# Constant matmuls in TensorE's pauses at the borders of the spectral stage and of the last stage of a four-layer convolution kernel

## The reference, cut to what matters

```python
x = x + _L0_conv_ref(_gn(x), ...)   # 1x1 channel mixing, leaky relu, then (y - min) / (max - min) per channel
x = x + _L1_conv_ref(_gn(x), ...)   # rfft2, a 3x3 complex convolution over the frequencies, bias, irfft2
x = x + _L2_conv_ref(_gn(x), ...)   # x rounded to int8 steps, 3x3 convolution, scale and bias
x = x + _L3_conv_ref(_gn(x), ...)   # circular 3x3 convolution
```

## Time and profile before

| what | value |
|---|---|
| time, median of 3 runs | 6660.71 us (6643.02 to 6668.57) |
| the profiled execution: its own time | 6655.92 us |
| its span, first to last instruction | 6653.9 us |
| TensorE matmul busy | 5695.1 us, 86% |
| VectorE busy | 4982.8 us, 75% |
| ScalarE busy | 4486.0 us, 67% |
| mean granted TensorE clock | 0.952 |

### The profile page before, as it was taken

The page is one execution under the profiler, slowest core; times in us unless marked ns, Lnnn a source line. Parts: engine busy times, 40 slices in busy tenths (PEclk is TensorE's granted clock), DMA queues, the critical chain, the costliest instruction groups (busy, mean ns, idle before and its releaser), DMA issues. The chain is left out here.

```text
span 6653.9 us, 202054 instructions
## 1 busy us (share of the span) xinstructions
PE 5695.1 (86%) x64138; PEld 3662.2 (55%) x64138; DVE 4982.8 (75%) x9849; ACT 4486.0 (67%) x8680; POOL 2750.1 (41%) x4633
## 2 busy tenths in 40 slices
PE   0259989989988988988998997994889889889889
PEld 0027757757756766765775774872334334334334
DVE  6867887887887887877887887788667667667664
ACT  0367766766767767767766556555878778778776
POOL 2136555556556646546556555650111111111112
PEclk9979999999999999999999998998999999999999
DMA  5325634633643652651661551553667667667665
GB/s 177 121 59 151 185 101 129 185 123 110 185 141 92 186 159 74 185 177 56 184 188 35 143 140 38 143 143 60 170 164 202 166 172 207 170 163 207 165 173 137
DMA packets 535618, 959.15 MB, mean 144 GB/s; under 512 B 121946, under 2 KB 126682, under 8 KB 532826
## 3 DMA queue, kind: packets, MB, share of 16 engines
q1 hardware_dynamic: 471898, 815.99, 44.0%
q10 hardware_dynamic: 63104, 134.23, 6.5%
HBM read 560.66 MB, written 287.60 MB: 127 GB/s over the span
## 5 line engine op out<-in xcount | busy, mean ns | idle before, releaser
L1575 PE MATMUL pC<-xs,taps 128*128 128x512 f16 x4608 | 1094.2, 382 | 108.1 <-DMA xhalo<-xs 100.4
L872 PE MATMUL pM<-gw,xh 64*128 64x256 f16 (+1 forms) x24960 | 1126.1, 244 | 0.0
L872 PEld LDWEIGHTS pM<-gw,xh 64*128 64x128 f16 x24960 | 964.6, 95 | 129.1 <-issue 2.9
L607 POOL TENSOR_TENSOR X<-X,zo 128x256 f32 (+1 forms) x512 | 371.9, 726 | 1243.5 <-DVE X L1019 1243.5
L1575 PEld LDWEIGHTS pC<-xs,taps 128*128 128x128 f16 x4608 | 448.4, 98 | 670.9 <-DVE xs L1624 88.3
L1471 POOL TENSOR_TENSOR xn<-xn,one_col 128x1 f32<-128x1 f32 x520 | 175.2, 337 | 1367.4 <-ACT xn L1505 1367.4
L778 PE MATMUL pM<-X,mix0s 64*64 64x512 f32 x2304 | 533.1, 638 | 179.8 <-DVE X L991 108.2
L592 POOL TENSOR_TENSOR X<-X,rl 128x512 f32 x384 | 478.2, 1274 | 397.0 <-ACT rl L638 396.7
L1491 ACT ACTIVATE scaled<-X,qbias,qscale 128x512 f32 (+1 forms) x512 | 410.9, 804 | 338.8 <-DMA X<-after_layer 277.8
L1513 ACT ACTIVATE xs<-xn 128x1028 f16<-128x1028 f32 x520 | 545.7, 1049 | 89.3 <-POOL xn L1472 88.7
L1019 DVE SCALAR_TENSOR_TENSOR X<-pZ,X 128x512 f32 (+1 forms) x512 | 353.8, 691 | 327.6 <-ACT zo L667 326.4
(11 more groups left out here) (236 smaller groups left out, 13781.1 us busy)
## 6 DMA issues: line engine op xcount, KB each, us to landing
gw<-row_weights SPq DMA_DIRECT2D x520, 288.0 KB, 3.4
after_layer<-X SPq DMA_DIRECT2D x512, 256.0 KB
out_dram<-result SPq DMA_DIRECT2D x512, 256.0 KB
stage<-in_x_dram SPq DMA_DIRECT2D x224, 512.0 KB
X<-in_x_dram SPq DMA_DIRECT2D x448, 256.0 KB
X<-after_layer ACTq DMA_DIRECT2D x224, 512.0 KB, 5.7
xhalo<-xs SPq DMA_DIRECT2D x504, 96.4 KB, 3.8
qhalo<-q SPq DMA_DIRECT2D x496, 96.2 KB, 4.0
```

The lines of the kernel that those rows point to most:

```text
L607: nc.gpsimd.tensor_tensor(X[:, j, 0], X[:, j, 0], zo[:, k], ALU.add)
L872: nc.tensor.matmul(pY[:, r, col:col + nd * P], row(xh, r)[:, k, p, ri, off:off + P], weights(r, q_, d, nd, ri), start=ri == 0 and off == 1 ...
L1575: nc.tensor.matmul(bank, taps3[:, d, wh], xs[:, h, own, d:d + W], start=d == 0 and n == 0, stop=False)
```

## The change

A helper `warm` is added to each of the two TensorE programs: n matmuls on constant operands that wait for no semaphore and set none. In the first program they read the table `inv_odd` and write half a bank of `pT` or `pZ` (a half that the next real matmul into it starts anew); in the second they read the weights `taps3` and write a new bank, `pIdle`, that nothing reads. Real matmuls, other engines and DMAs stay as they are. The places:

- 12 matmuls (256 columns) ahead of `small(n)` of each image,
- 40 (256 columns) between `mix(b, 3)` and `mix(b, 4)`,
- 36 (256 columns) behind `small(n + 3)`, ahead of the first transpose,
- 2 (512 columns) behind each of the conv2 of tiles 54 to 63, where conv3 has no tile any more,
- 8 (512 columns) ahead of the statistics matmul of the second program and 36 behind it.

```diff
+                    def warm(bank, n):
+
+                        for _ in range(n):
+                            nc.tensor.matmul(bank, inv_odd[:, 0, 0, 0:P], inv_odd[:, 0, 1], start=True, stop=True)
...
                         n = b * SMALL + 2
+                        warm(pT[:, HALF:W], 12)
                         small(n, pS[0:2, 0:P], ext[:, :], ident[:, :])
                         small(n + 1, pS[:, 0:2], ext_rows[:, :], ident[0:2, 0:2])
                         for j in range(J):
+                            if j == 4:
+                                warm(pT[:, HALF:W], 40)
                             mix(b, j)
...
                         small(n + 3, pS[:, 1:2], gmean1[:, :], mv[:, 1:2])
+                        warm(pZ[:, HALF:W], 36)
                         for i in range(ITEMS + 3):
...
+                pIdle = ps("pIdle", [P, W], pm)
...
+                    def warm(n):
+
+                        for _ in range(n):
+                            nc.tensor.matmul(pIdle[:, :], taps3[:, 0, 0], taps3[:, :, :].rearrange("p d h o -> p (d h o)")[:, 0:W],
+                                             start=True, stop=True)
+
                     def stats(b):
+                        warm(8)
                         pe.wait_ge(stats_in, b + 1)
                         nc.tensor.matmul(pS[:, 0:2], gmean2[:, :], mv[:, :], start=True, stop=True).then_inc(stats_out, 1)
+                        warm(36)
...
                             if c2 and live(w, 0, J):
                                 conv2(b + 1, w, k, g)
+                                if isinstance(v, int) and v > J:
+                                    warm(2)
```

## The result

The changed kernel takes 6691.3 us (median of 5 runs, 6689.1 to 6706.8), the kernel before 6660.7 us in its 5 runs. The ratio is 1.0051, with a 95% interval of 1.0031 to 1.0071. That lies in the predicted range of 6638 to 6700 us, but 23 us above the point of 6668, and at the border of what was called no change.

What follows compares the result with a forecast made beforehand. TensorE was taken to bound the steady parts, VectorE the mixing, and chains through other engines the borders. The terms +24.5 - 10 - 2 = +12.5 us on 6655.9 us gave 6668.4 us, range 6638 to 6700 us.

Steps and rivals of the forecast that it cites:

- What bounds the kernel: TensorE sets the pace in the steady parts, VectorE in mixing without slack, chains through other engines at the borders.
- The twelve: Ahead of `ext`: they take 2.5 us at the low clock, hidden in the wait with 0.5 us left.
- The credit for the clock at `ext`: The clock may rise inside the twelve, quickening the small matmuls and first tiles: 0 to 0.6 us an image.
- The forty: Between mixing tiles 3 and 4: not hidden, +3.5 us in seven images, +24.5 us; bounds +10 to +32.
- The rival in which they are hidden: Mixing tile 4 was late anyway, so only the gains stay: 6644 us; chance 0.10 together with no effect.
- the rival of low-clock fillers: Fillers run at the low clock, the forty +55 us, sum 6726 us; chance 0.16 with other costs of that size.
- The thirty-six at the spectral start: Ahead of the first transpose: no cost, 1.2 us gained an image, -10 us in all; bounds -23 and 0.
- 2.8 us: that is the most: Spectral start followed step by step at the high clock: first products end 2.8 us sooner, the most an image gains.
- The row that was called to agree: An image with a 10.2 not 13.6 us low stretch reached the next `ext` in 420.74 not 423.50 us.
- The last stage: Fillers behind each late conv2 and around the statistics: -2 us for the whole stage; bounds -18 and +15.
- The sum: All places together: +24.5 - 10 - 2 = +12.5 us, giving 6668.4 us.
- The rule: Half of all low-clock time counts as lost, whatever the engine does: 639 us of low clock cost 320 us.

Runs made afterwards that it cites:

- no_forty: The changed kernel without the forty fillers between mixing tiles 3 and 4: 6664.6 us (11 runs), ratio 1.0008 to the kernel before.
- edge: The changed kernel without the forty, the twelve moved to the end of the loop's body, ahead of its branch: 6650.3 us, one run.
- hold: The changed kernel without the forty, 54 instead of 36 fillers ahead of the first transpose, 12 and 5 more in the next two pauses: 6654.2 us, one run.
- first_only: The changed kernel with only the first program's fillers (12, 40 and 36), the second program as before: 6681.6 us (5 runs), ratio 1.0037.
- last_only: The changed kernel with only the second program's fillers, the first program as before: 6658.9 us (11 runs), ratio 1.0006.
- combo_border: The changed kernel without the forty; 54, 12, 5 at spectral start, 54 behind second-program statistics, pauses around an image's last pairs filled: 6626.9 us, ratio 0.9948.

## Why the prediction was right or wrong, point by point

**What bounds the kernel** held: steady parts kept their pace, and a delay of VectorE in the mixing stage went onto the end (no_forty).

**The twelve: this step failed.** The prediction said "hidden, with 0.5 us left", from a pair that ends and a wait that follows. The twelve start 1.86 us behind the pair in place of at once, so they end 1.4 us behind `ext`. In the kernel before, the same delay at the loop's end lay unseen inside the wait of 3.10 us for `ext`: the trace gave the wait its last releaser, and I took the whole of it for room. At the first border that trace shows idle time of this kind bare (the row at 924.27), and I had not read it. It cost +9.2 us, where the sum had none; edge shows it by moving the twelve ahead of the branch. The credit for the clock at `ext` was right: no_forty's mixing is (597.5 - 592.7) / 7 = 0.7 us shorter an image than before, and hold's, with the same twelve, less than 0.1 us (597.2), against 0 to 0.6.

**The forty** were right in mechanism and nearly in size: +24.5 us forecast, +21.3 with the credit in it measured (+27.6 in first_only's trace, where the clock was low at `ext` in five of the seven images and not in two). The rival in which they are hidden is out (26 us by no_forty), and the rival of low-clock fillers too, in which they cost +55. Both clocks at `ext` occur: with it low, 89.5 to 90.5 us; with it high, 87.6 to 87.8, +2.5 on 85.2 and not the +1.4 that the prediction had for that case. The forty start 5.0 us behind `ext`'s matmul there (4.55 forecast), take 4.54 us (4.4), and VectorE's second group starts 1.24 us behind the start of tile 4's matmuls (0.96). So the second group comes 10.72 us behind `ext`'s matmul, against 8.49 before and 12 in the forecast; with the clock low it comes 12.8 to 13.5 us behind. The first image shows nothing (136.6 for 136.3 us), as said.

**The thirty-six at the spectral start**: -10 us forecast, -3.2 measured, with the wait of 2.32 us behind them as forecast. For a pause left open 1.2 us an image was too much: 0.4 measured in this profile, and 0.4 to 0.9 over the six profiles that have this filler. For a start wholly at the high clock, "2.8 us: that is the most" was too little: 3.4 in six of hold's images. The step followed the clock's gain up to the first products and no further. The row that was called to agree, 420.74 in place of 423.50 us, agreed by the choice of its partner. 423.50 is the one image of the kernel before in which the way from statistics to `ext` was 16.60 and not 15.68 us; from first transpose to statistics the two are 405.07 and 406.90 us, so the shorter low stretch was worth 1.8 us and not 2.8.

**The last stage**: -2 us forecast; last_only's ratio gives +4 us, with -2 to +10 as its interval. That the thirty-six are hidden, with the halo at its old time, and that the clock falls again before the first conv3, came as said.

**The sum.** 24.5 - 10 - 2 = 12.5 stood against 21.3 + 9.2 - 3.2 = 27.3 us, which the two traces show in the first program, and 30.6 us between the medians. That the time came out inside the predicted range is in part luck: the range had room for 31.6 us, but no term of the sum was the twelve's. The 14.8 us between the two sums are the twelve's 9.2, the 6.8 that the starts gave less and the 2 counted for the last stage, less the forty's 3.2. The other 3 us between the medians have no place in a trace. The last stage's turns are 11.0 us longer in the profiled execution, and their spread from profile to profile covers that; neither is settled.

**The rule.** The Trainium skill, page "TensorE: Matmul & The Clock Gate", section "Terms", takes half of the throttled time as lost, and so of the 197 us that were taken away 98 should have come back. no_forty, at a clock of 0.968, has the clock's gain without the forty's cost, and its ratio is 1.0008: with the twelve's 9.2 us in it, the clock gave back some 4 us (11.9 by the mixing and the starts of its trace). With combo_border, 0.983 means 225 us low and 414 less than before. (The mean clocks are those of the profiled executions; over all its runs combo_border's was 0.981 to 0.983.) The rule would give 207 us, and the runs gave 36.4. The runs disagree with it here; TensorE spends much of these stretches waiting, busy for 4.0 of 17.1 us in the earlier trace rows.

## What to carry to other kernels

Ask of a filler what the engine behind it is waiting for: in a pause that a chain through other engines sets, it is free as long as it ends first, and ahead of work that a busy engine is about to want it costs what is left of its length beyond the lead that TensorE has there (some 1.4 us of the forty's 4.5 were free with the clock high, none with it low). What the clock pays is read behind the pause: only low time in which the following work runs counts. Closing the starts whole took all of it away and gave 3.0 us an image, while a pause left half open kept most of it and gave 0.4 to 0.9. At the first conv3, whose next turn waits for halo rows by DMA, a high clock gave nothing that the runs can tell. And a wait that the trace names by its last releaser may hide other delays, such as a loop's end, so put the filler ahead of the branch and not behind it.

## What the hardware showed that I had not expected

- TensorE stood 1.86 us between the last matmul ahead of the loop's end and the first behind it, with nothing to wait for in the profile, in a loop whose body has some 7,000 matmuls (1.7 to 2.2 us at five other borders of after, 4.3 us at the first). In edge, where the branch lies in a wait, it costs nothing at six of the seven borders.
- When the pause ahead of the spectral start shrank from 6.3 to 2.3 us, the low stretch of most images shrank from 13.6 to 10.2 us, but began later and ended only 0.7 us sooner behind the first transpose; with the pause at 0.4 us and the next ones filled it was gone in all eight images.
- Raising the mean clock from 0.952 to 0.983 made this kernel 0.5% faster, and raising it to 0.967 with forty of the fillers in a wrong place made it 0.5% slower. The mean clock says little about the time.
